# Other portions in the three tables that merge a second stream of work into layer 1

## The reference

```python
x = x + L0(gn(x))   # mLSTM block (12 heads of 32), linear, 3x3 convolution, BatchNorm over all 16 images, leaky ReLU
x = x + L1(gn(x))   # 6 heads: 6 numbers per token -> angles -> two 6-qubit circuits -> q, k of 4 numbers;
                    # softmax over 1024 tokens of -(|q|^2 + |k|^2 - 2 q.k) / tau, times v (32 channels), gated
x = x + L2(gn(x))   # 3x3 convolution gives 18 offsets per pixel; bilinear samples at 9 moved places,
                    # weighted per channel and place, and summed
x = x + L3(gn(x))   # 1x1 convolution to 510 channels, 2x2 FFT with a filter, depthwise 3x3 to 2x510, gelu(x1) * x2, 1x1 back
```

## Time and profile before

| | us |
|---|---|
| three runs | 9004.13, 9012.65, 9023.79 |
| median | 9012.65 |
| span of the profiled execution (first to last instruction) | 8833.4 |
| median less span (start and end of a launch, which the trace does not hold) | 179 |
| layer 0, all images: 0 to 3459.3 | 3459.3 |
| layer 1 of image 0, alone: to 3722.8 | 263.5 |
| layer 1 of image 1, with table k=0: to 4008.0 | 285.2 |
| layer 1 of images 2 to 14, table k=1: to 8150.9 | 4142.9 |
| layer 1 of image 15, table k=2: to 8472.5 | 321.6 |
| tail: to 8833.4 | 360.9 |

### The profile page before, as it was taken

One profiled execution on the slowest core, in us unless ns is written; L12 is line 12 of the kernel. 1 busy time (PEld: TensorE's weight loads), 2 busy tenths in 40 slices (PEclk: granted clock), 3 DMA queues, 4 the chain that ended last, 5 costly groups with the idle time before them and its releaser, 6 DMA issues.

```text
span 8833.4 us, 95654 instructions
## 1 busy us (share of the span) xinstructions
PE 7445.8 (84%) x35246; PEld 3495.5 (40%) x35246; DVE 5679.0 (64%) x9661; ACT 3844.7 (44%) x7430; POOL 2220.5 (25%) x1862
## 2 busy tenths in 40 slices
PE   7989889989989995668888888888888888888867
PEld 4544444445544452123333333333333333333343
DVE  4666656566665663457667667766766766766674
ACT  4444444444544552443543543444354354354330
POOL 1222222222222220012421421331231232133152
PEclk9999999999999996679899889899888888888988
DMA  1111111111111112024444544554444454354375
GB/s 64 35 38 37 36 37 38 40 38 44 42 42 38 41 38 72 4 78 118 153 141 107 169 150 112 149 163 116 133 152 129 117 160 144 97 167 146 99 220 145
DMA packets 244211, 849.75 MB, mean 96 GB/s; under 512 B 46413, under 2 KB 49177, under 8 KB 243361
## 3 DMA queue, kind: packets, MB, share of 16 engines
q1 hardware_dynamic: 150272, 388.71, 16.4%
q0 software_dynamic: 92160, 453.06, 16.2%
q10 hardware_dynamic: 1312, 1.87, 0.1%
HBM read 602.10 MB, written 89.68 MB: 78 GB/s over the span
## 4 chain that ended last, share of the span: by engine, by line
PE 39%; DVE 13%; ACT 6%; DMA 3%; issue 3%; SPq 2%; POOL 1%; DVEq 0%; ACTq 0%; POOLq 0%
PE ps L2189 10%; PE ps L2649 4%; PE ps L2434 4%; DVE arena L1901 4%; PE ps L2199 3%; PE ps L2660 2%; PE ps L2630 2%; PE ps L2127 2%; PE ps L2320 2%; SPq L2683 2%; PE ps L2113 2%; DMA arena<-arena 1%; DVE arena L400 1%; DMA arena<-img,arena 1%; PE ps L2152 1%
## 5 line engine op out<-in xcount | busy, mean ns | idle before, releaser
L2467 POOL DMA_INDIRECT arena<-img,arena x1152 | 1369.8, 1189 | 2685.6 <-DMA img<-arena 1859.8
L2364 DVE SCALAR_TENSOR_TENSOR arena<-arena 128x384 f32<-128x384 f32 x1152 | 748.0, 649 | 656.6 <-DMA arena<-img,arena 653.6
L1901 DVE TENSOR_REDUCE arena<-ps 128x2 f32<-128x1024 f32 x768 | 894.3, 1216 | 322.6 <-PE ps L2168 319.6
L2042 ACT ACTIVATE arena<-ps 128x512 f32<-128x512 f32 x1536 | 817.5, 603 | 315.1 <-PE ps L2199 312.4
L2189 PE MATMUL ps<-arena 128*64 128x512 f32 x3072 | 935.7, 711 | 0.0
L982 POOL TENSOR_TENSOR arena<-arena 128x512 f32<-128x512 f32 x384 | 442.1, 1158 | 1942.5 <-DMA arena<-decay 1942.4
L2649 PE MATMUL ps<-arena 128*64 128x512 f32 x3072 | 808.1, 651 | 129.6 <-DMA arena<-arena 73.9
L2434 PEld LDWEIGHTS ps<-arena 128*96 128x96 f32 x4608 | 557.9, 174 | 202.1 <-issue 201.7
L2434 PE MATMUL ps<-arena 128*96 128x128 f32 x4608 | 610.4, 289 | 26.3 <-DVE arena L2353 26.2
L1115 DVE TENSOR_TENSOR arena<-ps,arena 128x512 f32<-128x512 f32 x384 | 265.4, 691 | 492.3 <-issue 270.5
L949 PE MATMUL ps<-arena 128*128 128x512 f32 x1152 | 507.2, 596 | 0.0
(11 more groups left out here) (344 smaller groups left out, 12092.7 us busy)
## 6 DMA issues: line engine op xcount, KB each, us to landing
arena<-arena SPq DMA_DIRECT2D x1024, 144.5 KB, 2.9
arena<-decay SPq DMA_DIRECT2D x384, 256.0 KB, 3.2
img<-arena SPq DMA_DIRECT2D x162, 384.0 KB, 2.6
arena<-img,arena POOLq DMA_INDIRECT x1152, 4.5
arena<-y SPq DMA_DIRECT2D x16, 768.0 KB, 6.4
arena<-x SPq DMA_DIRECT2D x16, 768.0 KB, 6.3
out<-arena SPq DMA_DIRECT2D x16, 768.0 KB
arena<-x SPq DMA_DIRECT2D x16, 512.0 KB, 5.1
```

The source lines that it names most:

```text
L1901: dve.tensor_reduce(out, self.wides[B.at("max", b, g, n, h) // 2].rearrange("p (a b) -> p a b", a=2), AX.X, AL.max).then_inc(*S.mark("max_ ...
L2042: act.activation(self.p[n % 6], B("score", b, n)[:, :], ACT.Exp).then_inc(*S.mark("p_act", b, n))
L2364: dve.scalar_tensor_tensor(gb[:, 0:384], gb[:, 384:768], pp[:, 1, n:n + 1], gb[:, 0:384], AL.mult, AL.add).then_inc(*S.mark("corner_x", b, n))
L2467: pool.indirect_dma_start(self.g[n % 6], None, img, bass.IndirectOffsetOnAxis(ap=ii[:, n:n + 1], axis=0)).then_inc(*S.landed(f"{self.tag}g ...
```

## The change

The three tables and their starts are filled anew. Nothing else differs; line numbers stay.

```diff
--- before.py
+++ after.py
@@ -2696,13 +2696,13 @@
 
 
 NX = 3
-START = (-70, -40, -39)
-PACE = ("5400002103093700013600007001109209996000400000000007020621002011"
-        "2053100202000000033643000000000000002411100100901000000412000010",
-        "5000001123201010201423061000504220400010401121212314223330012011"
-        "1331111003000000033300000000082000200411100101710100000403000002",
-        "5000000222300020101234070200043200320123000222112134223321012011"
-        "1502111021000000034270000010000000241330013320500100300501100074")
+START = (-60, -38, -41)
+PACE = ("5281201820023121001010342210311213123310023010021321112023301212"
+        "2200113134010111111301210102005016112011122000000011100300102021",
+        "2000100232102101002234051020423111300020015211221332222321012011"
+        "1223111010100000112122201002031100002420020000612000200120002202",
+        "0211101203112121212332201113111221111112211212131211312213202102"
+        "1213211210101401220025000121311012011111220021410011121311141040")
 
 
 def build(nc, dram, NB, lay, debug=()):
```

## The result

The changed kernel takes 9090.6 us (median of 4 runs, 9060.62 to 9101.53) against 9010.74 us (4 runs, 9004.13 to 9023.79): the medians lie 80 us apart. The ratio made from the single runs is 1.0075, with a 95% interval of 1.0053 to 1.0097, which is 68 us (48 to 87). The forecast was 9082 us and slower, 69 us above before. The sum came out right; what it is made of was not quite, and one number that stood under it was misread. From here on a difference in us is the ratio less one, times the median of before; where the medians themselves lie otherwise apart, that is said.

The account below looks back on a forecast made before the run. TensorE, 84% busy, was taken as the bound, with 44.8 us idle per middle image. The items sum to +5.3 us per image, 69 us for 13; added to the 9012.65 us median, 9082 us. Range 8980 to 9150 us.

Parts of the forecast that it names:

- Item 1: Step 119: 6 instead of 24 matmuls cover the bank's emptying; 2.07 us wait plus 1.5 us clock, +3.6 us per image.
- Items 2 and 3: Step 101: 18 instead of 24 covering matmuls, +0.6 us per image; steps 110 to 112: cover kept, 0.
- Items 4 to 6: Per image: GroupNorm, position 118 moved, +0.6 us; circuits, position 129, +1.1; position 131 behind steps 16 and 17, +0.8.
- Item 7: Steps 34 to 54, rows and first maxima: maxima start about 6.4 us later, mostly absorbed by VectorE; +1.5 us per image.
- Item 8: Steps 65 to 67, second maxima: positions 58 and 59 fill waits on reductions; -1.9 us per image.
- Items 9 and 10: Per image: steps 81 to 86, row transposes in smaller portions, -1 us; slopes moved from step 73 to 80, 0.
- Images 1 and 15: 0 for each: image 1 gains 9.8, loses 11.8 us, bounds ±10; image 15 +4 and -4, bounds ±8.

Follow-up runs that it names:

- before again: The unchanged kernel before, with no edit, timed and profiled anew: 9021.32 us, ratio 1.0005 to itself, with a span of 9042.2 us.
- k02_only: The kernel before with only the tables and starts of images 1 and 15 from the changed kernel: 9043.03 us, ratio 1.0035.
- k2_only: The kernel before with only the table and start of image 15 from the changed kernel: 8992.54 us, ratio 1.0030.
- k1_only: The kernel before with only the table and start of images 2 to 14 from the changed kernel: 9059.14 us, ratio 1.0052.
- the one short execution: The first profile of the unchanged kernel before: a span of 8833.4 us, while its timed runs lie at 9004 to 9024 us.
- k1_rows: The kernel before with only the portions at steps 29 to 53 of images 2 to 14 from the changed kernel: 9009.39 us, ratio 1.0038.
- gate2: The kernel before with gather 10 of images 0 to 14, and those queued behind it, held until step 92's stretch ends: 9164.84 us, ratio 1.0168.

## Why the prediction was right, and where it was not

The parts of an image, in us per image over images 2 to 14: the forecast by the prediction's items beside what the traces show. Each length is from the end of TensorE's last layer-1 matmul of one part to that of the next. Old: mean of three profiles with the old middle table (before again, k02_only, k2_only); new: mean of two (the changed kernel, k1_only).

```
steps      items   forecast   old    new    measured
0-27       4,5,6     +2.5     69.5   70.0    +0.5
28-54      7         +1.5     84.2   86.5    +2.3
55-69      8         -1.9     51.9   51.1    -0.9
70-73      -          0        4.5    4.5     0.0
74-91      9,10      -1.0     44.2   44.3    +0.1
92-100     -          0       25.2   24.5    -0.6
101-109    2         +0.6     15.0   16.2    +1.2
110-118    3          0       19.0   18.0    -1.0
119-127    1         +3.6     16.1   18.0    +1.9
sum                  +5.3    329.6  333.1    +3.5
```

The differences are taken before rounding. Their sum is 46 us for 13 images, beside the 47 us of k1_only's runs. A row is a length: where a portion moved from one part to another, its work moved with it.

**Item 1, step 119.** The mechanism is as forecast. Step 119 of image 9 in the changed kernel, first TensorE, then ScalarE:

```profile
6681.59 0.90 PE L2434 MATMUL ps<-arena 128*96 128x128 f32 x6
6684.21 0.39 PE L2199 MATMUL ps<-arena 32*128 32x512 bf16 x2 [1.73 <-ACT arena L2049]
...
6681.73 0.59 ACT L2048 ACTIVATE arena<-ps 32x512 f32<-32x512 f32 x1 [1.68 <-PE ps L2189]
...
6683.57 0.59 ACT L2049 ACTIVATE arena<-ps 32x512 f32<-32x512 f32 x1
```

A hole of 1.73 us stands where 2.07 was forecast; TensorE's 6 matmuls took 0.90 and not 0.72 us. The clock costs what was said, too: images 8 and 4 have the same hole, at 1.00 and at 0.91.

```profile
6354.40:6371.10 16.70, 14.97 (x86) 6.50 (x85) 8.22 (x17) 10.63 (x20) 10.09 (x9) 1.00 0.54 178
5012.20:5030.50 18.30, 16.56 (x86) 7.89 (x84) 10.45 (x21) 10.63 (x20) 11.37 (x9) 0.91 0.57 188
```

The difference is 1.6 us; the forecast took 1.5. (The Trainium skill's rule, TensorE: Matmul & The Clock Gate, Terms, half of the throttled time, gives 18.3 x 0.09 = 1.6 us here: at this depth the trace agrees with it.) The stretch was to take "about 18" us and takes 18.0, and the clock was below 1.00 there in 9 of 13 images of the changed kernel. What was wrong is the number that it was set against: 14.5 us stood in the one short execution, and 15.5 to 16.5 is what this stretch takes otherwise. The term is about 1.9, not 3.6.

**Items 2 and 3, steps 101 and 110.** +1.2 and -1.0 against +0.6 and 0. The first is above its upper bound of 1. The forecast hole is there, 0.4 us in most images where 0.64 was forecast; the rest is other waits of up to 2.4 us and, in the changed kernel, a clock below the forecast 1.00 in 6 of 13 images. At 110 TensorE's one hole, a wait for ScalarE's exponentials (line 2042), shrank from 1.9 to 2.3 us to 1.4 in every image, where the prediction took it as unchanged. Neither was tried by a run of its own.

**Items 4 to 6, steps 0 to 27.** Steps 16 to 27 (circuits) +1.2, steps 0 to 15 -0.8. Two of the three small terms were taken at or near their upper bounds, and none below zero. Their sum was five times too large.

**Item 7, first maxima.** The delay was forecast at 6.4 us and is 7.2, and VectorE's slack took up some 5 us of it, as said. 2.3 us are left by these lengths and 2.6 by the runs of k1_rows, where I took 1.5, within the bounds of 0 and 6.4. This is the largest term of the loss by a little, and not item 1: the order of the terms was wrong.

**Item 8, second maxima.** -0.9 against -1.9. The waits of line 2168 on line 1901 were to shrink in the second maxima, and did, by 0.6 us per image. Over both maxima of images 2 to 14 they did not; before, profiled again:

```profile
PE ps L2168 <- DVE arena L1901: 83.6, 106, 1.3
```

and changed:

```profile
PE ps L2168 <- DVE arena L1901: 86.9, 140, 1.3
```

More waits, each shorter: what the second maxima won, the first lost (0.8 us per image). **Items 9 and 10.** The parts change as forecast, in opposite ways (74 to 82: 25.1 to 21.3 us; 83 to 91: 19.1 to 23.0 us), and cancel to +0.1. The hole at the bank's emptying is there in the waits of TensorE over images 2 to 14 of the changed kernel,

```profile
PE ps L2199 <- ACT arena L2049: 58.1, 39, 2.6
```

a wait that isn't among the eleven largest of before, profiled again. The tail stayed at 362 us, as forecast.

**Images 1 and 15: the step that failed.** "I take 0" for both, with bounds of 10 and 8 us. Image 15 lost 27 us by the runs and 20 by its length, three times its bound. The prediction weighed two crossings (transposes right behind the slopes, +4; step 92's cover, -4). The first is there at about its price, 1.70 + 1.60 us of waits; the stretch of 92 took 24.1 instead of 26.8 us, in a spread of several us. What was not looked for is the rest: the products put right behind their weighing (6.9 us of waits), the reductions waited for 5.1 us longer, and small waits over most of the parts. A table of which nearly every digit changes was judged by two of them. How the 20 us divide among these was not tried. For image 1, 31 - 27 leaves 4 us, less than the two runs can tell. Its lengths say 8: the slopes' place gave 8.4 us back at steps 74 to 82 (forecast: 9.8), and steps 83 to 109 took 16.8, of which 7.7 are in the stretch of 92, which varies from 17.9 to 28.3 us with the old table.

So 69 + 0 was forecast, and 47 + 31 came, beside 68 by the runs of the whole change. That the total was met is luck: two errors of opposite sign. (The text ahead of the prediction gives 6 as the largest portion of image 1's new table; it is 8, ahead of step 2. Nothing rests on it.)

**The span.** "179 us more" was put between span and time, as the start and the end of a launch. These are 1.8 us. The error did no harm to the sum, since it was added to the median, but it spoiled every comparison of parts with the first trace.

## What to carry to other kernels

A portion of a second stream has two prices: the wait that it no longer covers, where one comes once per stage (here the emptying of a held bank, and a chain of reductions that starts late), and the wait that it meets itself where it comes right behind its own producer. Look for those places in each table by itself. How even the portions are told nothing here: with two places restored, the finer table stood at 0.9997 of the old one (0.9979 to 1.0015). And before a trace is used as the measure of what a part takes, set its span against the runs' times: where they lie 2% apart, the trace is of another execution than the one being timed.

## What the hardware showed that was not expected

Beside a burst of gathers, ScalarE waits for TensorE's matmuls long after the trace shows them done, up to 12.38 us in one piece, and TensorE then waits for ScalarE. In the stretch of step 92 that is 8.6 us per image on average (25.8 against 17.2); with a third of the gathers left out, the whole kernel takes 1.6% less.

The trace of before, profiled again, shows which signal is late. In the stretch of 92 of images 2 to 14, ScalarE's first emptying activation starts 4.2 us on average behind the modelled end of the last matmul that it waits for; in the first profile it is 0.07 us. In 12 of the 13 images it starts within 0.03 us of an update of line 2189's semaphore in the trace. In image 9 that update stands at 6607.76, while the matmul ended at 6596.52. The way back is not late: in all 13 images TensorE's next score starts 0.06 us after ScalarE's fourth activation. So TensorE's completions reach ScalarE late. Whether the matmul itself ends later than the modelled end, or its signal is held up, the trace can't tell. (It holds 1421 of this semaphore's 1536 updates, the first profile's all of them, so a single missing event proves nothing.)

The Trainium skill (Runtime: NRT & Kernel Launch, Instruction fetch mechanics) says that engines refill their instructions over DMA queues of their own and that this is mostly hidden. A refill that queues behind gathers could look like such a stall, but it isn't what happens here. The trace shows refills as packets of the kind "instruction", on queues 8 and 14; the gathers are on queue 0. In the stretch of 92 of image 8 (6261.5 to 6292.0, 30.5 us, with 8.71 us of idle ScalarE in one piece) there is none; the queues of 6245 to 6292:

```profile
q0 software_dynamic: 1760, 8.65, 54.8%
q1 hardware_dynamic: 643, 1.97, 12.7%
```

Elsewhere in that execution no refill took longer than 1.8 us, and around the stretches of 92 they stand at the same places of the program as in the first profile, which has no such stall.

How many gathers run beside a stretch does not decide by itself. The same stretch with the same 14 took 29.6 us in one execution and 17.0 in the first profile of before. In gate2 the burst runs through the whole stretch of 101, which took 23.5 to 32.0 us in eleven images, but 15.8 and 16.4 in images 4 and 13. (A longer stretch also holds more gathers, so their count is no measure of the cause.) What differed in the short execution, and how the gathers delay TensorE's completions, stays open.

The three groups differed by 0.5% for the same kernel (8965.94 to 9013.44 us), more than several effects here; only ratios within a group were used.
